# Graph network on 12,500 nodes: the scalar-scalar products of the update turned round, with their sums on TensorE

## What is computed

```python
a0, a1 = agg[:, :64], agg[:, 64:].reshape(n, 32, 3)        # sums of the messages
xs, xv = x[:, :64], x[:, 64:].reshape(n, 32, 3)
u0 = einsum('nu,nv,uvw->nw', xs, a0, Wu_ss) * c0 + einsum('nui,nvi,uvw->nw', xv, a1, Wu_vv) * c1
u1 = einsum('nu,nvi,uvw->nwi', xs, a1, Wu_sv) * c2 + einsum('nui,nv,uvw->nwi', xv, a0, Wu_vs) * c2
u0, u1 = u0 + xs @ Lu_s * c3, u1 + einsum('nui,uw->nwi', xv, Lu_v) * c4
x = layernorm(2 * x + concat(u0, u1))
```

## Time and profile before

| | before |
|---|---|
| median of 3 runs | 8949.41 us |
| lowest and highest | 8934.07 and 8959.56 us |
| span of the profiled execution, which is its time here | 8954.3 us |
| TensorE matmul, busy | 6109.6 us (68%) |
| TensorE weight load, busy | 4449.2 us (50%) |
| DVE, busy | 5971.5 us (67%) |
| ScalarE, busy | 3773.2 us (42%) |
| GpSimd, busy | 5607.7 us (63%) |

### The profile page before, as it was taken

One profiled execution on the slowest core, in us unless ns is written; L12 is line 12 of the kernel. 1 busy time (PEld: TensorE's weight loads), 2 busy tenths in 40 slices (PEclk: granted clock), 3 DMA queues, 4 the chain that ended last, 5 costly groups with the idle time before them and its releaser, 6 DMA issues.

```text
span 8954.3 us, 133249 instructions
## 1 busy us (share of the span) xinstructions
PE 6109.6 (68%) x33695; PEld 4449.2 (50%) x33695; DVE 5971.5 (67%) x7512; ACT 3773.2 (42%) x11870; POOL 5607.7 (63%) x3978
## 2 busy tenths in 40 slices
PE   3555555555554777777777777777775777777777
PEld 2444344444443555555555555555553555455544
DVE  4555555555555766666666666666663888888888
ACT  1222222222222444444444444444443666666665
POOL 1555555555556255555555555555556999999999
PEclk6777777777777889888888888888887999999999
DMA  6666666666664355555555555555543222222221
GB/s 185 188 192 196 190 193 191 190 192 189 194 193 135 114 175 181 174 180 168 174 176 175 173 179 176 171 173 176 169 149 102 84 83 77 84 84 82 78 84 63
DMA packets 692540, 1372.60 MB, mean 153 GB/s; under 512 B 106047, under 2 KB 500077, under 8 KB 666863
## 3 DMA queue, kind: packets, MB, share of 16 engines
q10 hardware_dynamic: 84636, 590.82, 21.2%
q1 hardware_dynamic: 455091, 499.42, 18.6%
q0 software_dynamic: 152736, 281.45, 9.5%
HBM read 587.20 MB, written 784.08 MB: 153 GB/s over the span
## 4 chain that ended last, share of the span: by engine, by line
PE 36%; issue 18%; another core or an unknown queue 16%; DVE 11%; ACT 8%; POOL 7%; ACTq 1%; SPq 1%; DMA 1%; DVEq 0%; POOLq 0%
PE turn_ps L1200 7%; PE node_ps L1211 7%; PE prods_ps L1177 6%; POOL work L667 4%; DVE upd L983 3%; PE m_ps L1110 3%; POOL picks_sb L667 3%; DVE work L954 2%; PE node_ps L1224 2%; DVE upd L960 2%; ACT onehot L1581 2%; PE s_ps L1110 2%; PE s_ps L1092 2%; PE node_ps L1110 2%
## 5 line engine op out<-in xcount | busy, mean ns | idle before, releaser
L591 POOL DMA_INDIRECT slots<-pay,slot x3136 | 3090.5, 986 | 2087.2 <-issue 1519.2
L647 POOL TENSOR_TENSOR q<-xt,yv 125x3072 f32<-125x3072 f32 x200 | 1094.1, 5470 | 1079.8 <-PE turn_ps L1200 1044.6
L954 DVE TENSOR_TENSOR work<-prods_ps,xt 125x1024 f32<-125x1024 f32 x800 | 958.5, 1219 | 1179.0 <-remote 538.6
L1178 PE MATMUL prods_ps<-w_bil,ys_t 64*125 64x512 f32 x2400 | 1419.6, 688 | 5.6 <-issue 5.6
L1211 PEld LDWEIGHTS node_ps<-msgs,onehot 128*125 128x125 f32 x6800 | 975.8, 195 | 326.3 <-issue 299.5
L1211 PE MATMUL node_ps<-msgs,onehot 128*125 128x160 f32 x6800 | 1022.0, 311 | 159.4 <-ACT onehot L1581 147.1
L983 DVE TENSOR_REDUCE upd<-work 125x48 f32<-125x3072 f32 x300 | 1005.9, 3353 | 127.2 <-POOL work L667 120.3
L1575 ACT ACTIVATE onehot<-node_iota,msgs 128x125 f32<-128x125 f32 x3400 | 1028.5, 393 | 103.6 <-POOLq L635 73.2
L1177 PE MATMUL prods_ps<-w_bil,a_t 64*125 64x512 f32 x1600 | 865.0, 643 | 248.9 <-DVE work L954 159.9
L960 DVE TENSOR_REDUCE upd<-work 125x16 f32<-125x1024 f32 x800 | 949.6, 1208 | 0.0
L1177 PE MATMUL prods_ps<-w_bil,ys_t 64*125 64x512 f32 x800 | 551.8, 776 | 517.2 <-issue 280.9
(11 more groups left out here) (231 smaller groups left out, 11233.4 us busy)
## 6 DMA issues: line engine op xcount, KB each, us to landing
msgs<-slots ACTq DMA_DIRECT2D x200, 1428.0 KB, 6.1
slots<-zero ACTq DMA_DIRECT2D x183, 1386.0 KB
win<-table SPq DMA_DIRECT2D x784, 160.0 KB
picks<-picks_sb SPq DMA_DIRECT2D x196, 512.0 KB
picks_sb<-picks SPq DMA_DIRECT2D x196, 512.0 KB
table<-tab SPq DMA_DIRECT2D x200, 350.0 KB
slots<-pay,slot POOLq DMA_INDIRECT x3136
spill_in<-spill_sums SPq DMA_DIRECT2D x200, 80.0 KB, 2.0
```

The costliest lines, as they stand in the source:

```text
L591: g.indirect_dma_start(out=slots[layer][:, :], out_offset=bass.IndirectOffsetOnAxis(ap=slot[q][:, j:j + 1], axis=0), in_=pay[q][:, j, :], ...
L647: g.tensor_tensor(q3[0:HM, :].rearrange("p (i u v) -> p i u v", i=3, u=V), xt[nb][0:HM, S:D].rearrange("p (u i) -> p i u", i=3).unsqueeze( ...
L954: ve.tensor_tensor(third(r), prods_ps[r % 2][0:HM, :].rearrange("p (w u) -> p w u", u=S), X[:, 0:S].unsqueeze(1).broadcast_to([HM, ROUND / ...
L1178: te.matmul(prods_ps[r % 2][0:HM, 512:1024], ys_t[S:P, :], w.bil[S:P, 512 * r:512 * r + 512], start=True, stop=True).then_inc(s["prods"], 1)
```

## The change

**Scalar rounds turned.** In rounds 0 to 3 the weights are now the stationary side: four blocks of 128 weight columns a half against the turned sums `a2_t` (125 nodes as columns). The result has weight columns on partitions and nodes in columns, 2 x 4 x 125 = 1000 a round. `a2_t` and `x2_t` hold the sums and the features twice, on partitions 0 to 63 and 64 to 127.

**Multiply and sum.** DVE multiplies a round by `x2_t`, broadcast, into `zs` (new line 963). The four reduces (960) are gone. In their place TensorE sums over u in `scalar_sums` (new line 1240): 32 matmuls with a 32-column slice of `band`, a matrix with ones in two columns, each by 125 columns of `zs`; `tile_position` puts the four quarters of a round side by side in groups of 32 output columns. The result takes the buffer of a seventh round, hence RS_ALL = 7 and `prods_ps[(nb + r) % 2]`. ScalarE copies it (`scalars_out`), and one more matmul in the linear part adds it, put in order by `in_order`.

**Elementwise work.** In layer 0 GpSimd's outer product covers two components; DVE makes the third (`q_first`, new line 973) and both additions (`q_add`, new line 981), and a turn is 4 transposes, as in layer 1. In layer 1 DVE now does two components of the mixed rounds and GpSimd one (DIRECT = (3, 2)).

**Order and buffers.** In layer 1 both turns of q stand ahead of the edge sum; linear and `turn_y` change places and use `m_ps` and `s_ps`, and `turned_q` is first on ScalarE. In layer 0 both turns stand behind the edge sum. The turned features and sums are held twice, in the tile order's odd buffer in space of `spill_tab`. Some semaphores of the start are merged, and `band` and `in_order` are filled there.

The diff, with the indentation of the functions cut and plain renamings, the double `xa` and the merged semaphores left out:

```diff
-RS_ALL = R0 + R1
-DIRECT = (3, 1)
+RS_ALL = R0 + R1 + 1
+SUMS = R0 + R1
+QUARTER = ROUND // 2 // P
+BAND = 4 * R0 - 2
+Y_OUT = 3
+Q_PARTS = (3, 2)
+DIRECT = (3, 2)
...
+def row_sum(r, half):
+    return 4 * r + 2 * half
...
-ys = [sb(f"ys{b}", [P, 2 * S]) for b in range(2)]
+xa = sb("xa", [P, 2, 2, S])
...
-ys_t = sb("ys_t", [P, HM])
-a_t = sb("a_t", [S, HM])
-v_t = sb("v_t", [3 * V, HM])
+x2_t = [sb("x2_t0", [P, HM]), spill_tab[:, 0:HM]]
+a2_t = [sb("a2_t0", [P, HM]), spill_tab[:, HM:2 * HM]]
+v_t = [sb("v_t0", [3 * V, HM]), spill_tab[0:3 * V, 2 * HM:3 * HM]]
+ss_t = spill_tab[:, 3 * HM:4 * HM]
+zs = sb("zs", [P, R0, 2, QUARTER, HM])
...
-    g.tensor_tensor(q3[0:HM, :].rearrange("p (i u v) -> p i u v", i=3, u=V),
-                    xt[nb][0:HM, S:D].rearrange("p (u i) -> p i u", i=3).unsqueeze(3).broadcast_to([HM, 3, V, V]),
-                    yv[nb][0:HM, :, 0:V].unsqueeze(2).broadcast_to([HM, 3, V, V]), ALU.mult).then_inc(s["q_mul"], 1)
+    g.tensor_tensor(q3[0:HM, VV * i0:].rearrange("p (i u v) -> p i u v", u=V, v=V),
+                    xt[nb][0:HM, S:D].rearrange("p (u i) -> p i u", i=3)[:, i0:3, :].unsqueeze(3).broadcast_to([HM, 3 - i0, V, V]),
+                    yv[nb][0:HM, i0:3, 0:V].unsqueeze(2).broadcast_to([HM, 3 - i0, V, V]), ALU.mult).then_inc(s["q_mul"], 1)
...
+for q in range(QUARTER):
+    ve.tensor_copy(in_order[:, :].rearrange("p (r q e) -> p r q e", q=QUARTER, e=2)[:, :, q, :],
+                   ident[:, 32 * q:32 * q + 4 * R0].rearrange("p (r e) -> p r e", e=2))
+ve.memset(band[0:S, BAND:BAND + 1], 1.0)
+ve.memset(band[S:P, BAND + 1:BAND + 2], 1.0)
...
+    def scalars(r):
+        ve.wait_ge(s["prods"], RS_ALL * n + r + 1)
+        ve.tensor_tensor(zs[:, r, :, :, :],
+                         prods_ps[(nb + r) % 2][:, :].rearrange("p (h c) -> p h c", h=2)[:, :, 0:QUARTER * HM].rearrange("p h (q n) -> p h q n", n=HM),
+                         x2_t[nb][:, :].unsqueeze(1).unsqueeze(1).broadcast_to([P, 2, QUARTER, HM]), ALU.mult).then_inc(s["prods_used"], 1)
+    def q_first():
         ve.wait_ge(s["x_in"][nb], 16 * nh + 16)
+        ve.wait_ge(s["y_out"], Y_OUT * n + Y_OUT)
         if within(n, 1, NT):
-            ve.wait_ge(s["upd"], RS_ALL * n)
-            ve.wait_ge(s["h_ready"], n)
-        ve.wait_ge(s["y_out"], 4 * n + 4)
-        def third(r):
-            return work[0:HM, ROUND * (r % 3):ROUND * (r % 3) + ROUND].rearrange("p (w u) -> p w u", u=S)
-        for r in range(R0 + 1):
-            if r < R0:
-                ve.wait_ge(s["prods"], RS_ALL * n + r + 1)
-                if r >= 3:
-                    ve.wait_ge(s["upd"], RS_ALL * n + r - 2)
-                ve.tensor_tensor(third(r), prods_ps[r % 2][0:HM, :].rearrange("p (w u) -> p w u", u=S),
-                                 X[:, 0:S].unsqueeze(1).broadcast_to([HM, ROUND // S, S]), ALU.mult).then_inc(s["prods_used"], 1)
-            if r == 2 and layer == 0 and within(t, 2, NT + 1):
-                inverse(layer, t - 2)
-            if r > 0:
-                ve.wait_ge(s["prods_used"], USES[layer] * n + used(layer, r - 1))
-                ve.tensor_reduce(upd[0:HM, ROUND // S * (r - 1):ROUND // S * r], third(r - 1), AX_X, ALU.add).then_inc(s["upd"], 1)
+            ve.wait_ge(s["q_turned"], 2 * n)
+        ve.tensor_tensor(q3[0:HM, 0:VV].rearrange("p (u v) -> p u v", u=V),
+                         xt[nb][0:HM, S:D].rearrange("p (u i) -> p i u", i=3)[:, 0, :].unsqueeze(2).broadcast_to([HM, V, V]),
+                         yv[nb][0:HM, 0, 0:V].unsqueeze(1).broadcast_to([HM, V, V]), ALU.mult).then_inc(s["q_part"], 1)
+    def q_add(i):
+        ve.wait_ge(s["q_mul"], n + 1)
+        ve.wait_ge(s["q_part"], Q_PARTS[0] * n + i)
+        ve.tensor_tensor(q3[0:HM, 0:VV], q3[0:HM, 0:VV], q3[0:HM, VV * i:VV * i + VV], ALU.add).then_inc(s["q_part"], 1)
...
+    if nodes and layer == 0:
+        scalars(0)
+        scalars(1)
+        q_first()
+        scalars(2)
+        scalars(3)
+        if within(t, 2, NT + 1):
+            inverse(layer, t - 2)
+        q_add(1)
+        mixed_mul(R0)
+        q_add(2)
+        mixed_sum(R0)
+        mixed_mul(R0 + 1)
+        mixed_sum(R0 + 1)
+    if nodes and layer == 1:
+        for r in range(R0):
+            scalars(r)
+        mixed_mul(R0)
+        mixed_mul(R0 + 1)
+        mixed_sum(R0)
+        if within(t, 2, NT + 1):
+            inverse(layer, t - 2)
+        mixed_sum(R0 + 1)
...
             te.wait_ge(s["prods_used"], USES[layer] * n + used(layer, r - 2))
+        elif within(n, 1, NT) and r == 0:
+            te.wait_ge(s["prods_used"], USES[layer] * n)
+            if layer == 1:
+                te.wait_ge(s["copied"], R1 * n)
         elif within(n, 1, NT):
-            te.wait_ge(s["prods_used"], USES[layer] * n - USES[layer] + used(layer, r + RS_ALL - 2))
-            if layer == 1:
-                te.wait_ge(s["copied"], R1 * n - R1 + r + 1)
-        upper = a_t[:, :] if r < R0 else ys_t[0:S, :]
-        te.matmul(prods_ps[r % 2][0:HM, 0:512], upper, w.bil[0:S, 512 * r:512 * r + 512], start=True, stop=True)
-        te.matmul(prods_ps[r % 2][0:HM, 512:1024], ys_t[S:P, :], w.bil[S:P, 512 * r:512 * r + 512],
-                  start=True, stop=True).then_inc(s["prods"], 1)
+            te.wait_ge(s["ss_out"], n)
+        to = prods_ps[(nb + r) % 2]
+        if r < R0:
+            for q in range(QUARTER):
+                o = 512 * r + P * q
+                te.matmul(to[:, HM * q:HM * q + HM], w.bil[0:S, o:o + P], a2_t[nb][0:S, :], start=True, stop=True)
+                mm = te.matmul(to[:, 512 + HM * q:512 + HM * q + HM], w.bil[S:P, o:o + P], a2_t[nb][S:P, :], start=True, stop=True)
+        else:
+            te.matmul(to[0:HM, 0:512], x2_t[nb][0:S, :], w.bil[0:S, 512 * r:512 * r + 512], start=True, stop=True)
+            mm = te.matmul(to[0:HM, 512:1024], a2_t[nb][S:P, :], w.bil[S:P, 512 * r:512 * r + 512], start=True, stop=True)
+        mm.then_inc(s["prods"], 1)
+    def scalar_sums():
+        if not nodes:
+            return
+        te.wait_ge(s["prods_used"], USES[layer] * n + used(layer, R0))
+        if layer == 1:
+            te.wait_ge(s["copied"], R1 * n + 1)
+        to = prods_ps[(nb + SUMS) % 2]
+        for r in range(R0):
+            for hh in range(2):
+                o = BAND - row_sum(r, hh)
+                for q in range(QUARTER):
+                    mm = te.matmul(to[32 * q:32 * q + 32, 0:HM], band[:, o:o + 32], zs[:, r, hh, q, :],
+                                   start=(r == 0 and hh == 0), stop=(r == R0 - 1 and hh == 1), tile_position=(0, 32 * q))
+        mm.then_inc(s["prods"], 1)
...
-            te.wait_ge(*((s["q_mul"], n + 1) if layer == 0 else (s["q_part"], 2 * n + 2)))
+            te.wait_ge(s["q_part"], Q_PARTS[layer] * n + Q_PARTS[layer])
             if layer == 0 and within(t, 3, NT + 1):
                 te.wait_ge(LS[1]["t_out"], t - 2)
         else:
             te.wait_ge(s["q_turned_out"], 2 * n + 1)
         for j in range(QC // 2):
             o = P * (j + part * QC // 2)
-            if layer == 1:
-                mm = te.transpose(turn_ps[:, HM * j:HM * j + HM], q3[0:HM, o:o + P], idn)
-                continue
-            for i in range(3):
-                mm = te.matmul(turn_ps[:, HM * j:HM * j + HM], q3[0:HM, VV * i + o:VV * i + o + P], idn, start=(i == 0), stop=(i == 2))
+            mm = te.transpose(turn_ps[:, HM * j:HM * j + HM], q3[0:HM, o:o + P], idn)
...
-        if within(t, 2, NT):
-            te.wait_ge(s["lin_out" if layer == 0 else "h_ready"], t - 1)
+        if layer == 0 and within(t, 2, NT):
+            te.wait_ge(s["lin_out"], t - 1)
+        if layer == 1 and within(t, 1, NT):
...
+        if layer == 1 and within(n, 1, NT):
+            te.wait_ge(s["h_ready"], n)
+        to = (node_ps, m_ps)[layer]
+        te.matmul(to[0:HM, 0:D], ident2[0:HM, 0:HM], xt[nb][0:HM, :], start=True, stop=False)
+        te.matmul(to[0:HM, S:D], v_t[nb][:, :], w.lin_u[:, :], start=False, stop=False)
+        te.matmul(to[0:HM, 0:S], x2_t[nb][:, :], w.lin0[:, :], start=False, stop=False)
         for j in range(QC):
-            mm = te.matmul(node_ps[0:HM, 0:S], q_t[:, j, :], w.vv[:, j, :], start=False, stop=(j == QC - 1))
-        mm.then_inc(s["lin"], 1)
+            te.matmul(to[0:HM, 0:S], q_t[:, j, :], w.vv[:, j, :], start=False, stop=False)
+        te.wait_ge(s["ss_out"], n + 1)
+        te.matmul(to[0:HM, 0:S], ss_t[:, :], in_order[:, :], start=False, stop=True).then_inc(s["lin"], 1)
...
+    if layer == 1:
+        bilinear(0)
+        bilinear(1)
+        turn_q(0)
+        bilinear(2)
+        turn_q(1)
+        bilinear(3)
+        bilinear(4)
+        bilinear(5)
+        sum_edges()
+        scalar_sums()
+        turn_y()
+        linear()
+        return
     bilinear(0)
     bilinear(1)
     message(0, 0)
...
     bilinear(3)
     message(0, 3)
     bilinear(4)
-    turn_q(0)
     bilinear(5)
     sum_edges()
+    scalar_sums()
+    turn_q(0)
+    message(1, 0)
     turn_q(1)
```

(18 more changed lines are left out.)

106 lines of the change are left out of this document (52 added, 54 removed).

## The result

| | before | changed |
|---|---|---|
| median | 8949.33 us (4 runs) | 9135.41 us (4 runs, 9105.91 to 9150.77) |
| ratio | | 1.0204, 95% interval 1.0173 to 1.0235 |
| span of the profiled execution | 8954.3 us | 9129.2 us |

The change makes the kernel slower by 2%. The forecast was 8885, faster, so the direction was wrong. The time lies within the range only because the range took in the rivals, and close to the second rival (9140), though not by its mechanism, as will be seen.

A forecast was written before the change was run, and what follows sets the result against it. No engine full in layer 0's message tiles, GpSimd's scatters setting the pace; GpSimd and DVE nearly full in layer 1. 8954 + 220 (layer 1) - 276 (message tiles) - 10 (first tiles) = 8888, given as 8885; range 8640 to 9160.

The forecast's parts named there:

- the second rival: Slower, 9140 us: layer 0 keeps 12-scatter trains, low clock eats the edge sum's lead; layer 1 +2.6 a tile; chance 0.30.
- The loop is 21.05 us: Layer 1: turn of q, rounds 2 to 5, edge sum and outer product in one chain, 21.05 us against 20.8.
- +2.0: Layer 1: us a tile added for TensorE's clock falling in about half the cases or half the length.
- All tiles pay: Layer 1, worse case: by the skill's clock rule every tile pays for the low clock, up to +3.5 us.
- The edge sum starts earlier: Layer 0 message tiles: first turns go from ahead of the edge sum, sparing ScalarE's wait and copy: -2.8 us a tile.
- 35 to 36.5: Layer 0 message tiles: length in us a tile that would show the forecast right.
- the train: Layer 0: GpSimd's 12 scatters in a row, 15.1 us, would stop after 8: -1.3 us a tile.
- the hold: Layer 0 message tiles: while the scatters run, other engines see TensorE's work late; ScalarE's release 2.1 us after them.
- The release comes sooner, but more rounds remain after it: Layer 0: after 8 scatters engines resume sooner, with more rounds left: -1.3 us a tile, range 0 to -3.5.
- Additions over 2: Sign: DVE additions over 2 us would mean waiting for GpSimd that the forecast left out.
- The first rival: Layer 1 does not pay for the clock, layer 0 gains as forecast: 8693 us; chance 0.14.
- the third rival: Sums don't run side by side, 7.6 us; layer 1 tile 25.5, layer 0 +4 a tile: 9610 or more; chance 0.07.

The follow-up runs named there:

- e2: Changed kernel; layer 0's zero fills issued ahead of its sweep, 12 extra unused matmuls before layer 1's first turn of q: 8098 us, kernel before 7315.
- c2: The kernel before the change, unedited, run again in the second group: 7307 us, 28.2 us a message tile in layer 0.
- c1: The changed kernel, unedited, run again: 7853 us where the kernel before took 7312; 30.6 us a message tile in layer 0.
- e9: Changed kernel with eight extra unused matmuls directly ahead of layer 0's edge sum and layer 1's turns of q put back: 7136 us, kernel before 7313.
- e12: Changed kernel with ScalarE's last one-hot distances ahead of two message copies in layer 0, layer 1's turns put back: 8521 us, kernel before 9093.
- e5: Changed kernel, turns of q put back in both layers, DVE's second addition moved earlier in layer 0: 7040 us (before 7312); 8439 (before 9093).
- e3: Changed kernel with the old division of elementwise work in both layers: 8166 us, kernel before 7315.
- the first three groups: Three of five groups of follow-up runs, each run beside the kernel before, which took 7312 to 7315 us there.
- e4: Changed kernel with the 32 matmuls of the sums issued quarter by quarter in both layers: 8434 us, kernel before 7315.
- e6: Changed kernel with 14 extra unused matmuls behind layer 0's first two message parts, layer 1's turns put back: 7548 us, kernel before 7312.

## Why the prediction was wrong

The miss between the spans is 241 us (9129 for 8888): 84 in layer 1, 127 in layer 0's sweep, 30 at the start and in the passage. Layer 1 was drawn right and priced low; in layer 0 a step of the mechanism failed, and with it the sign of the forecast.

**Layer 1, drawn right and priced low.** "The loop is 21.05 us" and "+2.0" for the clock made +2.2 a tile; measured are +3.1, or 304 us instead of 220. By its parts: outer product to turn 10.4 as forecast; turn to edge sum 5.8 at the full clock for the forecast's 5.1, and 5.8 for 5.55 from the edge sum to the outer product, which with e2 makes 21.99 for the loop; and the clock 1.9 for 2.0. The 0.7 us between turn and edge sum lie in two places of e2's timeline: round 3 began 2.2 us after the turn and not 1.85, since the second turn waited for round 2 on TensorE, and round 5 took about 1.1 us, not 0.85. "All tiles pay" for the clock, which the forecast held for the worse case, fits e2 and the stage's 0.88. Of the signs, GpSimd (62%) and DVE (68%) under 80%, a pause before the turn and tiles of 22 to 24 us came; a clock under 0.85 did not (0.88).

**Layer 0 with messages, the step that failed: "The edge sum starts earlier".** The sum was -3.0 a tile; measured are -1.7 (38.6 to 36.9, over the "35 to 36.5" that was to show it), 159 us for the sweep and not 286. Averaged over the 85 tiles, from the starts and ends in the timelines: the outer product -1.77 (forecast -1.8); from its end to the start of the edge sum 24.96 to 22.83, -2.1, where the forecast had -2.8 for ScalarE's wait and copy and -1.3 for the train, together -4.1; the edge sum +0.96 (forecast +1.3); from its end to the next outer product +1.2 (+1.6). So the term that failed is the lead of the edge sum.

Without the hold this step has the wrong sign: from c2 to c1 the same stretch grew from 14.8 to 16.2 us. The forecast took the turns' copy out of ScalarE's way and let the edge sum follow round 5. But behind round 5 the edge sum met ScalarE's one-hot selections, which were late in their turn: the wait ahead of it grew by 1.6 us without the hold (0.6 to 2.2), and by 1.2 with it (1.3 to 2.5), and in that wait the clock fell. e9 measures what the clock costs there, 1.6 us a tile; that the wait itself can be taken away is seen in e12, for which there is only an estimate, 2 us a tile.

With the hold the train became 8 scatters, as forecast, and the release came 5.2 us sooner; but 3.1 us more passed between it and the edge sum: DVE now had all its products still to make, and 1.2 of it is the longer wait for the one-hots. "The release comes sooner, but more rounds remain after it" was right in kind; the forecast left out the one-hots. Why there is a hold, and only in some groups, stays open.

**The first tiles of layer 0** were to gain 1.1 us each, since DVE bounded them. They lost 2.2 (mean of six, 26.8 to 29.0; of the first five, 25.4 to 29.4), at a clock of 0.83 for 0.99. They are a loop of waits that runs through DVE as well: e5, with the turns and an addition moved, has 26.8, and e3, with the old division, 26.3 against 29.5 in c1. What it waits for most stays open.

**Small terms.** The sums took 1.91 us for the 2.5 that was taken, between the bounds 1.9 and 7.6. DVE's products of 1024 took 1.21 for 1.27. "Additions over 2" didn't come. Unforeseen was that h on DVE takes 0.33 us in layer 0 for the 1.7 of the earlier trace rows; there it stands beside no outer product any more. The 21 us at the start and 9 in the passage were given as under 2: the first h came at 2313 to 2330 us in the kernels of the first three groups that have the same start, and at 2315 in c2, so up to about 15 of it is scatter, and the rest stays open.

**The rivals.** The second rival's time, 9140, was met by luck: its trains of 12 did not come, layer 0 gained more than its 0.7 and layer 1 lost more than its 2.6, and the two errors cancelled. The first rival, that layer 1 does not pay for the clock, is refuted by e2, the third by the 1.91 us. In the third rival's sum the "+190" of layer 0 doesn't follow from its "+4" a tile; its 25.5 us for a tile of layer 1 agrees with e4's 25.6, but e4's sums took 5.8 us and not 7.6. The numbers leaned on the two gains in layer 0 as if they added up, and gave "slower" 0.39.

**Where the gain went.** Nothing was wrong with the new arithmetic. With turned rounds, sums on TensorE and the new division kept, and only the turns of q put back, layer 1 is 18.07 us a tile, 13% under before. DVE and GpSimd had been relieved, but the order had made one chain through all engines, in which neither was the bound.

## What to carry to other kernels

When an edit relieves the busy engines and at the same time moves a step in an engine's order, cost the two apart: draw the loop that runs once through each engine per tile, and see which work has newly come to stand inside it. An idle stretch of a few microseconds on TensorE can cost more than its length, because the passes after it run at half the clock (here 1.9 us after a pause of 4.1, and 1.6 after one of 2.2). If it can't be closed, filling it with matmuls that nobody uses shows by a single run what the clock costs; in a place without a pause they are only work (e6). After moving a step forward, ask which other producer its consumer waits for; here the edge sum only changed the one it waited for.

## What was not expected of the hardware

The same kernel took 8949, 9093 or 7312 us, under conditions that nothing in the program sets. In the sorting and message part before the sweeps (300 to 2300 us) the changed kernel of the first measurement moved 190 GB/s, and the same kernel in c1 243:

```profile
300.00:2300.00 2000.00, 1079.65 (x5222) 841.93 (x5223) 1125.03 (x2961) 517.81 (x1695) 1144.40 (x1134) 0.73 0.62 190
```

```profile
300.00:2300.00 2000.00, 1267.08 (x6801) 999.49 (x6799) 1457.27 (x3870) 663.98 (x2189) 1511.13 (x1491) 0.81 0.79 243
```

The change costs 2.0% in the one and 7.4% in the other. The hold of the earlier trace rows exists only where the transfers are slow (in c1 DVE takes up round 0 at 3811.7, 1.2 us after TensorE began it), and hides what the order does to TensorE: 0.88 of the clock in layer 0 in both kernels with it, against 1.00 and 0.91 without. So a time of this kernel is worth something only beside a run of its rival under the same condition.

64 passes of 32 output columns each took 1.9 us when neighbours in the order lay in different column groups, 5.8 when they lay in the same.

The sum h takes 1.7 us in layer 0 of the kernel before and 0.33 in its layer 1, and in both it stands beside GpSimd's outer product (7200 to 8700; layer 0 in the earlier trace rows):

```profile
L1000 DVE TENSOR_TENSOR h<-node_ps,upd 125x160 f32<-125x160 f32 x72 | 23.4, 325 | 7.5
```

The two differ in where an operand lies: `lin` in SBUF, `node_ps` in PSUM. With both operands in SBUF, h began 3.9 us after the start of the outer product on average and ended 0.18 to 0.22 us after its end, in each of the 85 message tiles: it waited for the outer product while it counted as busy.
